# First feed-forward block worked by halves of tokens in place of halves of the inner width

## The reference, cut to what matters

```
x (4, 256, 512)                     # tokens
w_gate, w_up  (1376, 512)           # ternary weights times one scale
w_down        (512, 1376)
```

## Time and profile before

| | before |
| --- | --- |
| median of 3 runs | 1546.58 us (1543.73 to 1546.64) |
| profiled execution, its time | 1543.49 us |
| its span | 1541.8 us |
| PE busy | 1374.1 us, 89% |
| DVE busy | 974.8 us, 63% |
| ACT busy | 459.4 us, 30% |
| POOL busy | 288.6 us, 19% |

### The profile page before, as it was taken

The page is one execution under the profiler, slowest core; times in us unless marked ns, Lnnn a source line. Parts: engine busy times, 40 slices in busy tenths (PEclk is TensorE's granted clock), DMA queues, the critical chain, the costliest instruction groups (busy, mean ns, idle before and its releaser), DMA issues.

```text
span 1541.8 us, 18547 instructions
## 1 busy us (share of the span) xinstructions
PE 1374.1 (89%) x6429; PEld 1060.3 (69%) x6429; DVE 974.8 (63%) x2208; ACT 459.4 (30%) x991; POOL 288.6 (19%) x170
## 2 busy tenths in 40 slices
PE   6699799999999998997976687788999899899998
PEld 5467577777777666876854365656888677678886
DVE  3677767868787865554588756875447677455142
ACT  3343324332443432421324100332221453222010
POOL 4110111111111111210212001312452331022120
PEclk9889899999999999999997699999999899799999
DMA  4412423233222321222213001310111100012001
GB/s 150 143 51 61 116 78 108 74 102 92 71 80 62 112 57 57 67 65 69 88 35 76 27 28 47 102 36 2 55 55 44 53 28 1 1 41 68 26 20 55
DMA packets 99389, 96.38 MB, mean 63 GB/s; under 512 B 13122, under 2 KB 72402, under 8 KB 99298
## 3 DMA queue, kind: packets, MB, share of 16 engines
q1 hardware_dynamic: 98786, 94.35, 21.0%
q0 software_dynamic: 512, 0.85, 0.2%
HBM read 84.34 MB, written 10.82 MB: 62 GB/s over the span
## 4 chain that ended last, share of the span: by engine, by line
PE 72%; DVE 18%; issue 3%; DMA 2%; ACT 2%; SPq 2%; POOL 1%; DVEq 0%; ACTq 0%
PE bank L1739 51%; PE bank L2109 6%; PE bank L1833 5%; DVE nf_y L1681 3%; PE bank L1823 2%; PE bank L2044 2%; PE bank L2064 2%; PE bank L1766 1%; DVE xn L1245 1%; DVE st L1318 1%; PE bank L2053 1%; PE bank L1824 1%; DVE xT L1201 1%; DVE rs L1212 1%; DVE st L1224 1%
## 5 line engine op out<-in xcount | busy, mean ns | idle before, releaser
L1739 PE MATMUL bank<-xT,slots 128*128 128x512 f32 (+1 forms) x1920 | 459.0, 396 | 5.0 <-DVE xT L1201 3.2
L864 POOL TENSOR_TENSOR slots<-staging,slots 128x1024 fp32r<-128x1024 f32 (+4 forms) x97 | 229.4, 2367 | 1074.5 <-ACT slots L961 1074.4
L1739 PEld LDWEIGHTS bank<-xT,slots 128*128 128x128 f32 (+1 forms) x1920 | 348.1, 182 | 102.2 <-issue 9.3
L1681 DVE TENSOR_SCALAR nf_y<-nf_w 128x512 fp32r<-128x512 f32 (+2 forms) x495 | 244.8, 523 | 29.7 <-PE bank L2109 28.4
L2109 PE MATMUL bank<-nf_y,nf_d 128*128 128x512 f32 (+2 forms) x495 | 164.2, 416 | 19.7 <-DVE nf_w L1691 11.7
L1739 PE MATMUL bank<-slots,h 128*128 128x512 f32 (+1 forms) x728 | 176.5, 401 | 4.5 <-DVE h L1344 4.5
L1739 PEld LDWEIGHTS bank<-slots,h 128*128 128x128 f32 (+1 forms) x728 | 139.0, 191 | 39.3 <-DVE h L1344 5.4
L961 ACT ACTIVATE slots<-staging 128x1024 fp32r<-128x1024 f32 (+4 forms) x97 | 98.1, 1018 | 189.5 <-PE bank L1739 175.5
L2109 PEld LDWEIGHTS bank<-nf_y,nf_d 128*128 128x128 f32 (+1 forms) x495 | 92.2, 192 | 59.2 <-issue 28.8
L995 ACT ACTIVATE e<-bank,mx 128x320 f32<-128x320 f32 x128 | 66.4, 523 | 211.0 <-DVE mx L1282 207.5
L1833 PE MATMUL bank<-eT,v 128*96 128x256 f32 (+1 forms) x384 | 111.1, 412 | 0.0
(11 more groups left out here) (251 smaller groups left out, 1678.0 us busy)
## 6 DMA issues: line engine op xcount, KB each, us to landing
staging<-in_L_wqkT SPq DMA_DIRECT2D x16, 480.0 KB, 3.7
nf_out<-nf_w SPq DMA_DIRECT2D x30, 256.0 KB, 2.1
staging<-nf_out SPq DMA_DIRECT2D x30, 256.0 KB, 2.9
staging<-in_L_woT SPq DMA_DIRECT2D x16, 384.0 KB, 3.7
staging<-in_L_w SPq DMA_DIRECT2D x12, 512.0 KB, 3.7
nf_r<-nf_rcp SPq DMA_DIRECT2D x40, 128.0 KB, 3.1
nf_a<-nf_max SPq DMA_DIRECT2D x40, 128.0 KB, 3.5
xn<-in_L_w SPq DMA_DIRECT2D x20, 256.0 KB, 3.9
```

What stands on the lines that cost most here:

```text
L864: g.tensor_tensor(lo, split_source(i), hi.bitcast(FP32), ALU.subtract).then_inc(*sig.mark("weight_low", i))
L1681: v.tensor_scalar(nf_y[0:rows, i % STAIR_RING, 0:size], w_, bound, first, compare, ALU.mult)\
L1739: ins = mm(dst, l_, r_, start=i == 0, stop=i == len(passes) - 1)
```

## The change

The loops change places. All 11 slices are now made for the first half of tokens, then all of w_down is multiplied for tiles 0 to 3, then the same for the second half. `h0` holds all 11 slices of 512 tokens. The four tiles of a half keep their PSUM banks from part 0 to part 1 (`begin`, `end` of `product`), so `acc0`, the copy to it and the sum go away, and ACT reads PSUM directly. Every chunk of the block is loaded and split twice: 34 chunks in place of 17. `turn(1, 1)` comes after two `up0` steps in place of one; `stats(2, 0)` and `turn(2, 0)` come with the first `up0` steps of the second half; `router1` moves there too. Context rows and small vectors of layer 1 have places of their own in SBUF and are loaded at the start of the block. The twelfth `up0` step's abs waits for the x of tile 3, since both use `f0`.

```
-    half_f = (FT + 1) // 2
-    steps += [("up0", 0, 0), ("turn", 1, 1), ("up0", 0, 1)]
-    steps += [("up0", f, hf) for f in range(1, half_f) for hf in range(2)]
-    steps += [("down0", 0, t) for t in range(TILES)] + [("router1",)]
-    steps += [("up0", f, hf) for f in range(half_f, FT) for hf in range(2)]
-    steps += [("down0", 1, t) for t in range(TPH)] + [("stats", 2, 0)]
-    steps += [("down0", 1, TPH), ("down0", 1, TPH + 1), ("turn", 2, 0)]
-    steps += [("down0", 1, t) for t in range(TPH + 2, TILES)]
...
+    steps += [("up0", f, 0) for f in range(2)] + [("turn", 1, 1)] + [("up0", f, 0) for f in range(2, FT)]
+    steps += [("down0", 0, part, t) for part in range(2) for t in range(TPH)] + [("stats", 2, 0)]
+    for f in range(FT):
+        steps += [("up0", f, 1)] + {1: [("router1",), ("turn", 2, 0)]}.get(f, [])
+    steps += [("down0", 1, part, t) for part in range(2) for t in range(TPH)]
+    steps += [("raw1", 1, 0), ("raw1", 1, 1), ("scores1", 1, 0), ("scores1", 1, 1), ("stats", 2, 1)]
...
-        for lo, hi in ((0, half_f), (half_f, FT)):
-            ffn_up("up0", cols(a["L0_wgT"]), cols(a["L0_wuT"]), lo, hi)
-            ffn_down("down0", lambda f, w: a["L0_wdT"][f * P:f * P + w], lo, hi)
+        for hf in range(2):
+            ffn_up(("up0", hf), cols(a["L0_wgT"]), cols(a["L0_wuT"]), 0, FT)
+            ffn_down(("down0", hf), lambda f, w: a["L0_wdT"][f * P:f * P + w], 0, FT)
...
-                elif s == ("raw1", 1, 0):
-                    sp.wait_ge(*sig.when("down0_product", (1, TILES - 1)))
+                elif s == ("up0", 1, 0):
+                    sp.wait_ge(*sig.when("o0_product", (2 * G0 - 1, TPH - 1)))
                     sp.dma_start(ctxN[:], a["ctx"].rearrange("b s d -> s b d")).then_inc(*sig.mark("loaded_ctxN", 0, 16))
...
+                if n == FT:
+                    act.wait_ge(*sig.when("x_done0", TPH - 1))
...
-            def down0(part, t):
+            def down0(hf, part, t):
                 if part == 0:
-                    act.wait_ge(*sig.when("down0_product", (part, t)))
-                    sc.activation(acc0[:, t], psum(("down0", part, t))[:], ACT.Copy).then_inc(*sig.mark("down0_part", t))
+                    return
+                act.wait_ge(*sig.when("down0_product", (hf, 1, t)))
+                n = hf * TPH + t
+                if t >= 2:
+                    act.wait_ge(*sig.when("x_done0", n - 2))
                 else:
-                    act.wait_ge(*sig.when("down0_sum", t))
-                    sc.activation(f0[:, t % 2, 1], f0[:, t % 2, 0], ACT.Abs, scale=256.0).then_inc(*sig.mark("dabs0", t))
-                    sc.activation(f0[:, t % 2, 2], f0[:, t % 2, 0], ACT.Sign).then_inc(*sig.mark("dsign0", t))
+                    act.wait_ge(*sig.when("h0_done", hf * FT + FT - 1))
+                sc.activation(f0[:, t % 2, 1], psum(("down0", hf, t))[:], ACT.Abs, scale=256.0).then_inc(*sig.mark("dabs0", n))
+                sc.activation(f0[:, t % 2, 2], psum(("down0", hf, t))[:], ACT.Sign).then_inc(*sig.mark("dsign0", n))
...
-                v.tensor_tensor(f0[:, t % 2, 0], psum(("down0", part, t))[:], acc0[:, t], ALU.add)\
-                    .then_inc(*sig.mark("down0_sum", t))
...
-            def down0(part, t):
-                user = ("down0_product", (part, t))
+            def down0(hf, part, t):
+                user = ("down0_product", (hf, part, t))
                 lo, hi = (0, half_f) if part == 0 else (half_f, FT)
-                pe.wait_ge(*sig.when("h0_done", 2 * hi - 2 + t // TPH))
-                bank = claim(("down0", part, t), ("down0_sum" if part else "down0_part", t))
...
+                pe.wait_ge(*sig.when("h0_done", hf * FT + hi - 1))
+                if part == 0:
+                    open_bank[t] = claim(("down0", hf, t), ("dsign0", hf * TPH + t))
+                pairs = [([h0[0:fwidth(f), f, t * P:(t + 1) * P]], down_chunk(("down0", hf), f, 0, user)) for f in range(lo, hi)]
+                product(open_bank[t][:], pairs, begin=part == 0, end=part == 1).then_inc(*sig.mark(*user))
```

More of the change, by code:

```diff
@@ L174, in schedule @@
             steps.append(("z1", t + 1))
-        steps.append(("zt1", t))
+        steps += [("gate1", t), ("zt1", t)]
         if t >= 1:
@@ L243, in schedule @@
         return steps
+    half_f = (FT + 1) // 2
     steps += [("up3", 0, 0), ("turn", 7, 1), ("up3", 0, 1)]
@@ L531, in ffn_up @@
                 w = fwidth(f)
-                chunk((name, f), P, (2, KT, w), [((0,), gate(f)), ((1,), up(f))], after=after_nf(name, FT + f))
+                chunk((*name, f), P, (2, KT, w), [((0,), gate(f)), ((1,), up(f))], after=after_nf(name, FT + f))
         def ffn_down(name, down, lo, hi):
@@ L538, in ffn_down @@
                 if w == P or n == 1:
-                    chunk((name, f), w, (n, D), [((i,), down(f + i, w)) for i in range(n)],
+                    chunk((*name, f), w, (n, D), [((i,), down(f + i, w)) for i in range(n)],
                           after=after_nf(name, 2 * FT + f + n - 1))
                 else:
-                    chunk((name, f), P, (1, D), [((0,), down(f, P))], after=after_nf(name, 2 * FT + f))
-                    chunk((name, f + 1), w, (1, D), [((0,), down(f + 1, w))], after=after_nf(name, 2 * FT + f + 1))
+                    chunk((*name, f), P, (1, D), [((0,), down(f, P))], after=after_nf(name, 2 * FT + f))
+                    chunk((*name, f + 1), w, (1, D), [((0,), down(f + 1, w))], after=after_nf(name, 2 * FT + f + 1))
         def after_nf(name, item):
-            return ("nf4_stored", item) if name in ("up3", "down3") else None
+            return ("nf4_stored", item) if name[0] in ("up3", "down3") else None
         def cols(ap):
@@ L958, in split @@
                     act.wait_ge(*sig.when(*known.user[("chunk", ring_names[slot_no[name] - NSLOT])]))
-                if after is not None and after[0] == "down0_product":
-                    act.wait_ge(*sig.when(*after))
                 sc.activation(weight(name, 0), split_source(i), ACT.Copy).then_inc(*sig.mark("weight_high", i))
@@ L1330, in cut @@
                 f = f0[0:p, n % 2]
-                twice, whole = f[:, 1].bitcast(INT32), f[:, 3].bitcast(INT32)
+                twice = whole = f[:, 1].bitcast(INT32)
                 link(v.tensor_scalar(twice, f[:, 1], 0.5, 256.25, ALU.subtract, ALU.min))
@@ L1738, in product @@
                         xt_ready(inputs, first[i])
-                    ins = mm(dst, l_, r_, start=i == 0, stop=i == len(passes) - 1)
+                    ins = mm(dst, l_, r_, start=begin and i == 0, stop=end and i == len(passes) - 1)
                 return ins
@@ L1857, in down_chunk, with down0 @@
                 first = lo + (f - lo) // 2 * 2
[L1858 to L1859 removed]
+                if (*stage, first) in chunk_no and f != first and (*stage, f) not in chunk_no:
+                    parts = need((*stage, first), user)
                     return [q[0:fwidth(f), 1] for q in parts]
[L1861 removed]
+                parts = need((*stage, f), user)
                 return [q[0:fwidth(f), 0] for q in parts]
[L1864 to L1865 removed]
+            def down0(hf, part, t):
+                user = ("down0_product", (hf, part, t))
                 lo, hi = (0, half_f) if part == 0 else (half_f, FT)
[L1867 to L1872 removed]
+                pe.wait_ge(*sig.when("h0_done", hf * FT + hi - 1))
[3 more added lines that the diff above has]
+                product(open_bank[t][:], pairs, begin=part == 0, end=part == 1).then_inc(*sig.mark(*user))
             def raw1(layer, b):
```

115 lines of the change are left out of this document (47 added, 68 removed).

## The result

| | time, us (median, range, runs) | ratio to before, 95% interval |
| --- | --- | --- |
| before, beside it | 1545.59 (1542.17 to 1547.44, 6 runs) | |
| changed | 1534.37 (1528.74 to 1539.76, 6 runs) | 0.9927 (0.9902 to 0.9952) |

Faster, by 11.2 us (0.7%). The profiled execution took 1528.74 us, 14.8 less than the profiled one of before. For what the block itself gives I use the trace: from the first `up0` product to the second `xn` transposes it took 238.83 us before and 228.70 after, 10.1 less. The rest of the span moved by more from profile to profile: the block began between 591.2 and 600.9 us in the twelve others, though ahead of it nothing was edited but the last loads of scales in four of them (e8 to e11).

The account below looks back on a forecast made before the run. PE was busy 201.8 of the block's 238.9 us, so gains came from 37.1 idle and lowered clock. Stretches 66.5 + 34.5 + 67.6 + 52.6, wait 2.0, half clock 3.5 gave 226.7, 12 less: 1534.5 us, range 1523 to 1547.

Parts of the forecast that it names:

- The total: Block from first `up0` product to second `xn` transposes: 226.7 us against 238.9; median 1534.5 us.
- First half, up: 11 `up0` steps and 16 transposes, with no wait at `turn(1, 1)`: 66.5 us.
- First half, down: w_down for the first half's tiles: 26.3 us work, waits of 3.5, 1.4 and 2.6, 0.7 drift; 34.5 us.
- the small split: Sixth w_down chunk (96x512), split only after part 0's last tile, holds up part 1's start by 1.4 us.
- Second half, up: 11 `up0` steps, transposes and router: 67.6 us, plus 2.0 of wait at `turn(2, 0)` in place of 6.99.
- Second half, down: Last stretch, to the transposes, set by DVE and SP: 52.6 us, with DVE idle for `nf_a` over 7 us.
- DVE finishes the slices at 6.5 us: Start of the second half's down stretch: DVE done with the last slices 6.5 us in; item 27's first step at 25.1.
- Here the chain is not PE's: Second half's down stretch: DVE's work and SP's issues and transfers, not PE, set its 52.6 us.
- The doubled weights: 17 more chunks, each 1.02 us on ACT and 2.37 on POOL; at most 35 us of DVE holds, mostly absorbed.
- Rival 2: Weights come too late: loads queue on SP behind `nf_r` or `nf_a`, 8 us a time; 1558 us, chance 0.09.
- Rival 1: Waits only move: down parts twice as often meet staircase, DVE's tail and SP's 16 us; 1544 to 1549, chance 0.12.
- Rival 3: Splits miss DVE, so the last part ends with PE rather than DVE; 1518 to 1526 us, chance 0.14.

Follow-up runs that it names:

- e8: Kernel before, with the scales of each w_down NF4 item loaded in five transfers instead of ten; 1534.07 us, ratio to before 0.9912.
- e11: As e10, with PE also waiting for the sixth w_down chunk only before a tile's last two products; 1522.58 us, ratio to before 0.9847.
- e1: Changed kernel with `turn(1, 1)` again behind one `up0` step instead of two; ratio to before 0.9956.
- e6: Changed kernel with PE waiting for the sixth w_down chunk only before the last two products that need it; ratio to before 0.9947.
- e3: Changed kernel with POOL writing only 8 columns of the low part of each second-half chunk, rest not computed; ratio to before 0.9833.
- e2: Changed kernel with `turn(2, 0)` directly behind `stats(2, 0)`, before the second half's first `up0` step; ratio to before 0.9986.
- e0: Changed kernel run and profiled again without any edit; 1532.79 us, ratio to before 0.9923.
- e4: Changed kernel with the second half's third w_down chunk split one `up0` step later; ratio to before 0.9915.
- e9: Changed kernel with the scales of each w_down NF4 item loaded in five transfers instead of ten; 1534.9 us, ratio to before 0.9917.
- e10: Changed kernel with both the five-transfer scales of e9 and the late split of e4; ratio to before 0.9887.

## Why the prediction was right, and where it was off

**The total.** 226.7 us were forecast for the block and 228.7 measured; the median 1534.5 and 1534.37. The second agreement is closer than the working deserves, and in part luck: the block gave 2 us less than forecast, and the rest of the program was some us shorter in the profiled execution (its time less the block is 1300.0, before 1304.7), which no step of mine explains and which varies between profiles anyway.

**First half, up: right.** No wait, full clock, 65.2 for 66.5. e1 shows that the second step of cover is what does it.

**First half, down: right in mechanism, each wait a little smaller.** 3.5, 1.4 and 2.6 us were forecast, at a sum for DVE, at the sixth chunk for POOL and at `nf_end` for SP; measured 2.81, 1.28 and 2.11, in that order and at those places. That the last of them is SP's shows on DVE, ahead of the `nf_end` that PE waits for:

```profile
682.39 1.58 DVE L1662 TENSOR_TENSOR nf_w<-nf_w,nf_r 128x512 f32<-128x512 f32 x1 [5.90 <-DMA nf_a<-nf_max]
```

The stretch took 36.6 for 34.5, for the most part because its half clock (4.15 for 2.98 in the tile behind the first wait, and 4.00 for 10 products behind the last) stands in another term of the sum. What my sum missed is how closely the two last waits hang together: e6 shows that the 1.28 cost nothing of its own, so the small split was not on the path, though the sum and the signs to look for had it there.

**Second half, up: right in length, by another mechanism.** 69.6 forecast with 2.0 of wait at `turn(2, 0)`, 71.0 measured. `xn` was ready when PE came to it; instead ACT's and DVE's backlog shows behind it, 1.66 for `g` and 1.01 for the router's result, and e3, where both waits are gone, ties them to POOL's splits. e2 bounds the cover from the other side: without it, 12.14 us.

**Second half, down: the mis-sized term.** 52.6 forecast, 55.9 measured. The step that failed reads "DVE finishes the slices at 6.5 us". It was 10.4. From there on the chain has the lengths of the forecast: item 27's first step 18.7 us later (18.6 forecast), and the transposes 26.8 after that (27.5 forecast). Its make-up is another: DVE was to stand idle for `nf_a` for over 7 us, and stood 3.51 (5.05 in e0), since it also waited 3.47, 0.68 and 1.97 us for PE on the way there. This sign did not come. The cause of the 3.9 us is ACT's wait of 4.98 with three splits in a row, and e4, which takes that stall away (and shifts the holds with it), has DVE through at 5.5 and the stretch at 52.59. I had counted the splits as busy time of ACT and POOL, and SP's round for the buffers as 8 us of 11.6, a mean over steps; but `spread_splits`, which places them in the order, puts three chunks of w_down behind one `up0` step of the second half, and there are two buffers. In the first half, where it puts two there and one behind the step after, ACT waits only 1.00 us.

"Here the chain is not PE's" was only half right. After e9 it must read: SP's chain and PE's, the latter delayed by the 6.02, ended within 0.1 us of each other in one profile, and SP's some 1.6 us later in the other.

**The doubled weights: right that they are hidden in the first up stretch** (PE 65.00 busy of 65.00, clock 1.00), and that they cost where DVE is short. e3 bounds that cost at 13 to 14 us for the second half's chunks, and 4.3 of them lie in the second up stretch, behind the stats, where the forecast saw the danger but its sum has nothing beyond the 2.0. Rival 2, weights too late, did not come about as a loss: PE's waits for POOL are 1.28 and 1.37, and 0.46 at the start of the last stretch. Yet the mechanism of the failed term is kin to it: a load that came late, though it was ACT and DVE that paid.

**Rival 1**, the waits only move, was right for one of them (the 6.02 in place of 6.99) and wrong in sum. **Rival 3**, splits that miss DVE, was wrong: four operations of DVE take 2.0 to 2.9 us in the last stretch behind its first cut.

**What the gain is made of.** e8 adds what the prediction could not see. With SP's chain shortened the old order takes 229.23 and the new 225.05: the change is then worth 4.2 us, not 10.1. So some 6 of the 10.1 us are the waits of the earlier trace rows for SP, which the new order meets less often, and 4 are the covers for `xn` and `h`, net of what the splits cost. The measured times of e8 and e9, 1534.07 and 1534.9, can't tell these 4 us; that split rests on the traces alone. With the late split as well (e10) the new order's block is 11.0 us below e8's; whether the old order has a stall of its own to give up was not tested.

## What to carry to other kernels

Where a wait is put down to a small transfer, count the issues ahead of it on its queue before reordering the work: halving the number of transfers of the scales gave the old order 9.6 us of its block, almost as much as the whole change. If a removed wait gives nothing, look for a second chain that ends at the same point; here two edits worth 3.35 and 3.65 us by their traces gave 10.5 together. And a step that is moved moves on every engine: look for what stands behind it on ACT and DVE too, and how many steps in a row ask for the same two buffers.

## What the runs showed of the hardware

- Issuing from SP costs by the transfer: ten of them 5.83 us, five that bring the same bytes in the same pieces 3.15. The Trainium skill, Perfetto Trace Analysis, "What 'DMA-bound' means", says that the issuing engine's track shows the making of descriptors, not the data's movement, and asks for large descriptors. That the row isn't the data's movement agrees with these runs; but the descriptors' pieces stayed the same size here, and fewer transfers alone brought the 2.7 us.
- Behind a wait PE's products are dearer, by an amount that I had put at 1.7 us each time. In the changed kernel 12 products took 4.15 us after the wait of 2.81 and 4.50 after that of 6.02, in place of 2.96, in stretches whose granted clock is 0.91 and 0.85; after the wait of 1.28 ten took 2.57. So these three waits cost 1.2, 1.5 and about 0.1 us beyond their own length. The price doesn't go by the wait alone: behind the wait of 2.11 ten products took 4.00 us at a granted clock of 0.58, and in e1, behind a wait of 2.12 at the same place, 2.49 at 1.00. Why the clock fell in one and not in the other, no run here shows.
- In these rows a DVE operation held by a split on POOL ends about when the split does, whatever its size: `h` and `x` took 2.71 to 2.85 us in place of 0.69, and an operation on 128x4 took 2.19 in place of 0.17. In the changed kernel this last one ended at 820.05 and the split beside it at 820.02.
